# Attention scores from two products over 128 rows instead of three, with queries and keys rearranged for it, in a cross-attention and mixture-of-experts kernel

## The reference, cut to what matters

```python
q, k, v = split(concat([layernorm(x), ctx]) @ W_qkv)      # q from x, k and v from ctx
dots    = einsum('bhqd,bhkd->bhqk', q, k) * 64 ** -0.5    # the scores, summed over d = 64
x       = x + softmax(dots) @ v @ W_out + b_out
x       = x + moe(layernorm(x))                           # 16 experts, the two best for each token
```

## Time and profile before

| | us |
|---|---|
| median of 3 runs | 596.6 (596.18 to 596.95) |
| the profiled execution | 594.73 |
| its span, first to last instruction | 592.9 |
| from the first scores of pair 3 (110.15) to those of pair 14 (393.26): eleven pairs | 283.11, so 25.74 a pair |
| mean granted clock of TensorE over the span | 0.969 of 2.4 GHz |

### The profile page before, as it was taken

The page is one execution under the profiler, slowest core; times in us unless marked ns, Lnnn a source line. Parts: engine busy times, 40 slices in busy tenths (PEclk is TensorE's granted clock), DMA queues, the critical chain, the costliest instruction groups (busy, mean ns, idle before and its releaser), DMA issues.

```text
span 592.9 us, 20076 instructions
## 1 busy us (share of the span) xinstructions
PE 521.4 (88%) x6712; PEld 445.6 (75%) x6712; DVE 521.9 (88%) x1496; ACT 481.5 (81%) x1364; POOL 464.1 (78%) x567
## 2 busy tenths in 40 slices
PE   2898999999999999999999999999866878999800
PEld 0577889898999998989898999998755656666600
DVE  5879999999999999999999999999998869877616
ACT  0897999999999999999999999999966565766600
POOL 8995766788898988989898898988884577777730
PEclk9998999999999999999999999999999898999965
DMA  9793165229306384930762393075503232333139
GB/s 272 203 319 69 14 196 194 46 51 331 91 11 180 86 264 135 325 87 12 211 209 45 66 327 88 13 230 189 120 20 83 68 90 82 105 91 96 48 128 315
DMA packets 69703, 81.64 MB, mean 138 GB/s; under 512 B 8116, under 2 KB 47564, under 8 KB 69604
## 3 DMA queue, kind: packets, MB, share of 16 engines
q1 hardware_dynamic: 56244, 67.60, 39.3%
q0 software_dynamic: 4352, 8.47, 4.3%
q10 hardware_dynamic: 9008, 4.30, 2.7%
HBM read 18.82 MB, written 46.31 MB: 110 GB/s over the span
## 4 chain that ended last, share of the span: by engine, by line
PE 71%; DVE 12%; ACT 6%; issue 5%; DMA 3%; ACTq 2%; POOL 0%; POOLq 0%; SPq 0%; DVEq 0%
PE bank L1385 17%; PE bank L1384 17%; PE bank L1386 16%; PE bank L1502 8%; PE bank L1550 5%; PE bank L1591 3%; DMA ctx_sb<-results 2%; ACTq L511 1%; ACT probs L612 1%; PE bank L1640 1%; DVE pT L1251 1%; PE bank L1624 1%; PE bank L1394 1%; PE bank L1529 1%; DVE qmax L1230 1%
## 5 line engine op out<-in xcount | busy, mean ns | idle before, releaser
L612 ACT ACTIVATE probs<-bank,nbias 128x128 f32<-128x128 f32 x512 | 146.0, 368 | 4.2
L1251 DVE TENSOR_TENSOR pT<-bank,pT 128x512 f16<-128x512 f32 x128 | 87.4, 683 | 9.1 <-ACT pT L631 6.6
L928 POOL DMA_INDIRECT results<-z,stage x72 | 71.2, 989 | 21.8 <-issue 13.4
L1230 DVE TENSOR_REDUCE qmax<-bank 128x4 f32<-128x512 f32 x128 | 87.0, 679 | 0.6 <-PE bank L1386 0.6
L1384 PE MATMUL bank<-keys,q_pad 128*128 128x128 f16 x480 | 86.6, 219 | 0.0
L1386 PE MATMUL bank<-keys,q_pad 128*128 128x128 f16 x480 | 86.6, 219 | 0.0
L1385 PE MATMUL bank<-keys,q_pad 128*128 128x128 f16 x480 | 86.6, 219 | 0.0
L814 POOL DMA_INDIRECT places<-payload,slots x64 | 65.8, 1029 | 22.5 <-issue 9.3
L1502 PE MATMUL bank<-ident,probs 128*128 128x128 f32 x512 | 78.3, 275 | 4.5 <-DVE pT L1251 3.9
L631 ACT ACTIVATE pT<-bank 128x512 f16<-128x512 f32 x128 | 78.1, 610 | 4.9 <-PE bank L1502 4.8
L1384 PE MATMUL bank<-xT,w_qkv 128*128 128x256 f16 x256 | 69.9, 273 | 1.1 <-DVE xT L974 0.8
(11 more groups left out here) (266 smaller groups left out, 1958.1 us busy)
## 6 DMA issues: line engine op xcount, KB each, us to landing
places<-z SPq DMA_DIRECT2D x8, 4160.0 KB, 14.9
q_pad<-q_nat SPq DMA_DIRECT2D x120, 128.0 KB, 2.4
stage<-places SPq DMA_DIRECT2D x64, 65.0 KB, 1.8
ctx_sb<-results SPq DMA_DIRECT2D x14, 256.0 KB, 4.7
ctx_sb<-in_ctx_dram ACTq DMA_DIRECT2D x4, 512.0 KB, 10.5
stage<-in_L_ffn_Wgu_dram SPq DMA_DIRECT2D x1, 2048.0 KB, 9.5
out_dram<-x_sb ACTq DMA_DIRECT2D x7, 256.0 KB, 5.8
stage<-in_L_xattn_W_qkv_dram SPq DMA_DIRECT2D x3, 512.0 KB, 6.3
```

The costliest lines, as they stand in the source:

```text
L612: last = nc.scalar.activation(probs[:, b, k, :], score_bank[b][:, k * P:(k + 1) * P], ACT.Exp, bias=nbias[:, b, k:k + 1], scale=exp_scale)
L928: nc.gpsimd.indirect_dma_start(out=results, out_offset=bass.IndirectOffsetOnAxis(ap=to, axis=0), in_=z[:, (q - 5) % NZ, t, :], in_offset=None,
L1230: nc.vector.tensor_reduce(qmax[:, r % 2, :], score_bank[r % 2][:, :].rearrange("p (h k) -> p h k", h=4), AX.X, ALU.max).then_inc(s["qmax_o ...
L1251: nc.vector.tensor_tensor(pT[:, r % 2, LO, :], pt_bank[:, :], pT[:, r % 2, HI, :], ALU.subtract).then_inc(s["pt_lo"], 1)
```

## The change

For pairs 1 to 15 the scores of a head become two products, both over 128 rows. `q_both` holds the high half of a head's queries in its own 64 rows and the low half in the 64 rows of the other head. `k_twice` holds the high half of the keys in both sets of rows, and `k_low` the low half of the keys in the head's own rows, with zeros in the others. So q_both x k_twice gives high x high and low x high, and q_both x k_low gives high x low.

```diff
--- before.py
+++ after.py
@@ -136,9 +136,11 @@
-        q_nat = sb("q_nat", [P, 2, 4, 2, 2, 256], F16)
-        q_pad = sb("q_pad", [P, 2, 2, 8, 256], F16)
-        keys = sb("keys", [P, 2, 2, 8, 256], F16)
+        q_nat = sb("q_nat", [P, 4, 2, 2, 256], F16)
+        q_both = sb("q_both", [P, 2, 8, 256], F16)
+        k_twice = sb("k_twice", [P, 2, 8, 256], F16)
+        k_low = sb("k_low", [P, 2, 8, 256], F16)
+        keys = sb("keys", [P, 2, 8, 256], F16)
...
-        DIRECT = (1, 4, 6)
+        DIRECT = (1, 4, 7)
         VIA = [t for t in range(8) if t not in DIRECT]
...
+        def first_item(t, half):
+
+            return (k_twice if t % 4 >= 2 else q_both)[:, half, blocks_of(t), :]
+
+        def qk_item(t, half):
+
+            if t % 4 < 2:
+                return q_nat[:, blocks_of(t).start // 2, half, :, :]
+            return keys[:, half, blocks_of(t), :]
...
+                def ready(t, low):
+
+                    if t in DIRECT:
+                        sp.wait_ge(s["act_split" if low else "act_high"], direct_before(q, t) + 1)
+                    else:
+                        sp.wait_ge(s["qk_split" if low else "qk_high"], copied_before(q, t) + 1)
...
+                halves_of = [tuple(slice(64 * k, 64 * k + 64) for k in (odd, 1 - odd)) for odd in range(2)]
                 for t in (4 * g, 4 * g + 1):
-                    if t in DIRECT:
-                        sp.wait_ge(s["act_split"], direct_before(q, t) + 1)
-                    else:
-                        sp.wait_ge(s["qk_split"], copied_before(q, t) + 1)
-                    blk = 4 * g + 2 * (t % 2)
-                    for odd in range(2):
-                        rows = slice(64 * odd, 64 * odd + 64)
-                        sp.dma_start(q_pad[rows, :, odd, blk:blk + 2, :],
-                                     q_nat[rows, q % 2, blk // 2, :, :, :]).then_inc(q_moved[g], 16)
+                    ready(t, True)
+                for odd, (own, other) in enumerate(halves_of):
+                    move(q_both, (own, own), q_nat, HI)
+                    move(q_both, (own, other), q_nat, LO)
+                for t in (4 * g + 2, 4 * g + 3):
+                    ready(t, False)
+                for odd, (own, other) in enumerate(halves_of):
+                    move(k_twice, (own, own), keys, HI)
+                    move(k_twice, (own, other), keys, HI)
+                for t in (4 * g + 2, 4 * g + 3):
+                    ready(t, True)
+                for odd, (own, other) in enumerate(halves_of):
+                    move(k_low, (own, own), keys, LO)
...
-                    wait(act, "score_mm", q * 8 - 8)
-                    if t in (1, 4) and q > 2:
-                        act.wait_ge(q_moved[t // 4], 64 * (q - 2))
+                    if t in (1, 4) and q > 1:
+                        act.wait_ge(q_moved[t // 4], 160 * (q - 1))
...
-            nc.gpsimd.memset(q_pad[64:128, :, 0], 0.0).then_inc(s["pad_zero"], 1)
+            nc.gpsimd.memset(k_low[64:128, 0], 0.0).then_inc(s["pad_zero"], 1)
...
-            nc.gpsimd.memset(q_pad[0:64, :, 1], 0.0).then_inc(s["pad_zero"], 1)
+            nc.gpsimd.memset(k_low[0:64, 1], 0.0).then_inc(s["pad_zero"], 1)
...
-                if t == 0:
-                    wait(pool, "score_mm", q * 8 - 8)
-                if t in (0, 5) and q > 2:
-                    pool.wait_ge(q_moved[t // 4], 64 * (q - 2))
+                if t in (0, 5) and q > 1:
+                    pool.wait_ge(q_moved[t // 4], 160 * (q - 1))
...
+                    to = score_bank[r % 2][:, k * P:(k + 1) * P]
                     if p == 0:
-
-                        a = [q_nat[rows, par, blk // 2, h, k % 2, tok] for h in range(2)]
-                        b = [keys[rows, par, h, blk, tok] for h in range(2)]
+                        a = [q_both[rows, h, blk, tok] for h in range(2)]
+                        b = [k_twice[rows, h, blk, tok] for h in range(2)]
+                        last = three(to, a[HI], a[LO], b[HI], b[LO])
                     else:
-                        a = [q_pad[:, h, odd, blk, tok] for h in range(2)]
-                        b = [keys[:, par, h, blk, tok] for h in range(2)]
-                    last = three(score_bank[r % 2][:, k * P:(k + 1) * P], a[HI], a[LO], b[HI], b[LO])
+                        nc.tensor.matmul(to, q_both[:, odd, blk, tok], k_twice[:, odd, blk, tok], start=True, stop=False)
+                        last = nc.tensor.matmul(to, q_both[:, odd, blk, tok], k_low[:, odd, blk, tok], start=False, stop=True)
                 last.then_inc(s["score_mm"], 1)
...
-                            pe.wait_ge(q_moved[r // 2], 64 * p)
+                            pe.wait_ge(q_moved[r // 2], 160 * p)
```

More of the change, by code:

```diff
@@ L252, in direct_before, with blocks_of @@
             return (q - 1) * len(DIRECT) + sum(k < t for k in DIRECT)
[L254 to L259, removed]
+        def blocks_of(t):
+            blk = 4 * (t // 4) + 2 * (t % 2)
+            return slice(blk, blk + 2)
+        def first_item(t, half):
[4 more added lines that the diff above has]
+            return keys[:, half, blocks_of(t), :]
         def by_two(m):
@@ L418, in move_q, with move @@
                 sp.wait_ge(s["score_mm"], q * 8 - 2 + 2 * g)
-                for t in (4 * g, 4 * g + 1):
-                    if t in DIRECT:
-                        sp.wait_ge(s["act_split"], direct_before(q, t) + 1)
-                    else:
-                        sp.wait_ge(s["qk_split"], copied_before(q, t) + 1)
-                    blk = 4 * g + 2 * (t % 2)
-                    for odd in range(2):
-                        rows = slice(64 * odd, 64 * odd + 64)
-                        sp.dma_start(q_pad[rows, :, odd, blk:blk + 2, :],
-                                     q_nat[rows, q % 2, blk // 2, :, :, :]).then_inc(q_moved[g], 16)
+                def ready(t, low):
[3 more added lines that the diff above has]
+                        sp.wait_ge(s["qk_split" if low else "qk_high"], copied_before(q, t) + 1)
+                def move(to, rows, source, half):
+                    some, k = ((2 * g, 2) if source is q_nat else (4 * g, 4))
+                    from_rows = source[rows[0], some:some + k, half] if source is q_nat else source[rows[0], half, some:some + k]
+                    to_rows = to[rows[1], odd, 4 * g:4 * g + 4, :]
+                    if source is q_nat:
+                        to_rows = to_rows.rearrange("p (b i) n -> p b i n", b=2)
+                    sp.dma_start(to_rows, from_rows).then_inc(q_moved[g], 16)
+                halves_of = [tuple(slice(64 * k, 64 * k + 64) for k in (odd, 1 - odd)) for odd in range(2)]
+                for t in (4 * g, 4 * g + 1):
+                    ready(t, True)
[11 more added lines that the diff above has]
+                    move(k_low, (own, own), keys, LO)
             sp.wait_ge(s["blank_ok"], 2)
@@ L768, in split_qk @@
                 wait(pool, "qk_copied", k + 1)
-                if t == 0:
-                    wait(pool, "score_mm", q * 8 - 8)
-                if t in (0, 5) and q > 2:
-                    pool.wait_ge(q_moved[t // 4], 64 * (q - 2))
-                nc.gpsimd.tensor_tensor(qk_item(par, t, HI), each, zeros[:, :].rearrange("p (i n) -> p i n", i=2),
+                if t in (0, 5) and q > 1:
+                    pool.wait_ge(q_moved[t // 4], 160 * (q - 1))
+                nc.gpsimd.tensor_tensor(qk_item(t, HI), each, zeros[:, :].rearrange("p (i n) -> p i n", i=2),
                                         ALU.add).then_inc(s["qk_high"], 1)
                 wait(pool, "qk_high", k + 1)
-                nc.gpsimd.tensor_tensor(qk_item(par, t, LO), each, qk_item(par, t, HI), ALU.subtract).then_inc(s["qk_split"], 1)
+                nc.gpsimd.tensor_tensor(qk_item(t, LO), each, qk_item(t, HI), ALU.subtract).then_inc(s["qk_split"], 1)
             inverse_root("stat_agg", 4, mv, var_eps, rstd, "rstd_ok", 2)
@@ L1048, in first_low @@
                 dve.wait_ge(s["first_high"], t + 1)
[L1049 to L1050 removed]
+                nc.vector.tensor_tensor(first_item(t, LO), first_bank[t % 4][:, :].rearrange("p (i n) -> p i n", i=2),
+                                        first_item(t, HI), ALU.subtract).then_inc(s["first_split"], 1)
             dve.wait_ge(s["wgT_mm"], 1)
```

10 lines of the change are left out of this document (4 added, 6 removed).

## The result

The changed kernel takes 608.94 us in the median of 6 runs (607.97 to 610.93), the kernel before 596.78 us on the same chip (596.18 to 597.53): a ratio of 1.021, with a 95% interval of 1.020 to 1.023. It is slower by 12.2 us, where I had forecast 3.7 us. The sign was right, and the size lies outside my range (592 to 605).

A forecast was written before the change was run, and what follows sets the result against it. PE was taken to set the pace before, and a loop from POOL through ACT to POOL after. Terms +4.1 - 1.8 + 0.8 + 0.6 = +3.7 us on 596.6 gave 600.3 us; range for 8 in 10: 592 to 605.

The forecast's parts named there:

- The loop from POOL through ACT to POOL: Pairs 3 to 13: a ring of POOL and ACT work, 26.11 us a pair against 25.74, giving +4.1 us.
- POOL from the split of item 0 to that of item 5, 294.70 to 309.73, without a wait for another engine: 15.03: The loop's last and longest term: POOL's work from item 0 to item 5, taken to stay at 15.03 us.
- No faster PE shortens it: Claim on the 26.11 us loop: it does not pass through the scores, so PE's saving of 1.79 us a pair cannot shorten it.
- hidden, at nothing: Ten moves per group: issued every 0.64 us, landing 2.4 us after issue, 1.3 us spare at step 0, so costing nothing.
- a sign of being wrong that I had named: Stated beforehand as showing the forecast wrong: PE's longest wait ending with a DMA in step 0 or 2.
- I take half: -1.8: Pairs 1 and 2: the loop is slack, PE's gain is 3.6 us at most, and half was counted, -1.8 us.
- pair 14, +0.8: Pair 14: shift comes 1.9 us later, an earlier copy of item 5 and a lighter POOL give some back, +0.8 us.
- ahead of pair 1, +0.6: Pair 0: nothing is removed, and its last moves, now ten, may come late for pair 1, +0.6 us.
- My sentence that PE's waits should not lower it: PE's clock: claimed to stay up despite waits, since from 430 to 460 PE is busy 19.98 of 30 us at 1.00.
- the forecast's own range: The range of the main case alone: 597.5 to 603.5 us, for a loop of 25.95 to 26.4 us a pair.
- the gain gets through: Rival: the loop is shorter than 25.74 us, DVE bounds next, -8.7 and -1.8 us, 586 us; chance 0.17.
- The moves come late: Rival: moves queue behind a clearing and PE stalls at step 0 in up to seven pairs, +7 us, 607; chance 0.10.

The follow-up runs named there:

- e1_items: The kernel before with one number changed, so that POOL splits item 6 ahead of root and shift and item 7 is split directly: 645.24 against 630.97 us, ratio 1.023.
- e7_before_between: The kernel before with items 1, 4 and 7 direct and root and shift between the halves of item 6's split: 629.2 against 627.47 us, ratio 1.003.
- f1_two_products: The kernel before with the product of the queries' low halves by the keys' high halves left out from pair 1 on: 592.71 against 596.18 us, ratio 0.993.
- f4_product_again: The kernel of f3_queries_two_buffers with the first score product issued twice from pair 1 on: 601.53 against 596.18 us, ratio 1.008.
- f3_queries_two_buffers: The changed kernel with root and shift between the halves of item 6's split and q_both double-buffered by pair: 594.09 against 596.18 us, ratio 0.995.

## Why the prediction was right in kind and wrong in size

**Right: that PE's gain doesn't come through, and why.** The loop from POOL through ACT to POOL is there, and the run with the item order alone (e1_items) and the one that puts `y` back in it (e7_before_between) show it by themselves. ACT starts `y` 4.94 us behind the scores of step 7 (291.52) and not 3.93 as in the earlier trace rows, one microsecond later, as worked out. The terms of that half hold to 0.13 us.

**Wrong, the step that failed: "POOL from the split of item 0 to that of item 5, 294.70 to 309.73, without a wait for another engine: 15.03", and with it "No faster PE shortens it".** I took a stretch that had no wait while the other part of the pair was shorter, and assumed that it would keep none. It measures 15.57, with 0.56 of waiting for ACT's copy of item 5. Before, POOL ran that stretch as its own bottleneck. Afterwards the late `y` delays the exponentials of step 7, these delay PE's scores of step 1 (298.67), the transposes behind them wait 0.68 us for DVE's `pT`, and in steps 3 to 5 PE waits for DVE some tenths more. So its step 5 comes 13.06 us behind step 1, with eight products a step, where it was 12.64 with twelve; then follow item 5's projection and ACT's copy of it, for which POOL waits. The loop has a branch through PE and DVE that my sum left out. PE's own work is a small part of it: with `y` late a pair takes 26.39 us with eight products and the moves relieved, and 26.62 with twelve and the old moves. The loop term was +0.37 us a pair (26.11), where 26.39 was measured with the moves relieved and 26.49 in the changed kernel: 0.65 from this loop and about 0.1 from the moves, +8.3 and not +4.1 in pairs 3 to 13.

**Wrong: the moves "hidden, at nothing".** I took an issue at 0.64 us, a group at 5.76 from first to last issue; groups take 5.8 to 7.5. I found 1.3 us to spare at step 0 and, at step 2, 0.4 us with PE dense or about 2 more "with PE's waits". Those 2 us were the late `y`'s. With `y` back, the moves took over at 26.36 us a pair. In the changed kernel PE's waits for them are few (3.4 us in all at L1502), but the longest that it has in pairs 1 to 14 is one of them, 1.49 us at step 2 of pair 2, and that was a sign of being wrong that I had named. In five of the eleven pairs 3 to 13 the scores of step 0 or step 2 start 0.25 us after the last landing. My sentence that they cost nothing was nearly true in these pairs, and only in the shadow of the other loop. Nor are the pairs alike, as I had said: they take 25.1 to 27.3 us, and 25.0 to 27.1 with the moves relieved. Why is open.

**Wrong: pairs 1 and 2, "I take half: -1.8".** It is +1.7. The saving gives 0.3 us there (52.01 us with two products and nothing else, against 52.34), as DVE is busy for 50.95 of it; and the moves cost most of the rest: 52.47 us with the first half's moves relieved and `y` still late, 1.6 less than the 54.05 as changed. The 1.49 us named above are in these pairs.

**Right: pair 14, +0.8** (measured +1.0). **Wrong: ahead of pair 1, +0.6,** and the measured -1.4 isn't the change's either. It is the clock: pair 0 takes 25.62 us in the profile of before, with a mean granted clock of 0.93 because 3.4 us of it from 51.1 on are at 1.2 GHz, and 24.06 in that of the changed kernel at 1.00; f1_two_products, without the new moves, has 24.13 at 1.00, and f4_product_again, with them, 25.64 at 0.93. At the same clock the moves cost nothing there. Unforeseen are +2.1 from the start of pair 15 to its step 7, and 2.0 us behind it. In the first the moves are as late as in other pairs, and the clock has its part: 0.94 over that stretch, with 3.4 us at 1.2 GHz from 447.7 on, against 1.00 before. My sentence that PE's waits should not lower it rested on one row; in e7_before_between, with the old products, the clock falls in that stretch too (0.87), so these profiles don't tell whether the change has to do with it. The 2.0 us don't look like the change's: that part is 149.99 us in the kernel before and 151.85 in f1_two_products, 151.94 in the changed kernel, 152.3 in f4_product_again. Why the one profile of before is the shortest is open.

**The range.** The lower end of the forecast's own range doesn't follow from its loop: 25.95 us a pair gives 11 x 0.21 - 0.4 = +1.9, so 598.5 and not 597.5. It changes nothing here.

**The rivals.** That the gain gets through (586) was excluded from the start: even alone it is worth 3.5 us. I had put its bound at DVE, which was the right place, but 8.7 us lower than today was far too much: no kernel here had DVE busy for more than 98% of these pairs. "The moves come late" came closest in its number (607), but by another mechanism: not behind a clearing, but by SP's own issue time, and with `y`'s loop beside it. Which of the two now holds the pairs of f3_queries_two_buffers at 25.58 us, DVE and ACT (98% and 96% busy) or the loops between them, no run separates.

## What to carry to other kernels

Before pricing a saving on the busiest engine, look at the next one: with PE at 99.8%, DVE at 97% and ACT at 97% of a stretch, a saving of 7% on PE was worth 0.7%, and leaving the work out in the old kernel is the run that shows it at once. When a loop is summed from a trace, a stretch without waits is a lower bound, not a length; ask which engines its inputs come from, and what delays them once the loop is longer. When an added piece of work makes a loop longer, look which loop it was: here two of them pass through PE. And mend suspected causes together as well as singly: two loops of 26.4 us each look innocent when only the other is removed.

## What the runs showed of the hardware

PE products of 128 columns follow each other at 0.056 us when their rows are the same, 64 or 128; where a product over 64 rows follows one over 128 or the reverse, the start comes at 0.15 to 0.16 us. A step with eight products and eight such changes cost 1.27 us, more than twelve products of one kind (0.67). What the lost 0.1 us goes with is in the rows of PEld above: in a run of equal rows a load starts 0.05 us ahead of its product, behind a change of rows it starts with it. Why it isn't earlier no run here shows. The Trainium skill (TensorE: Matmul & The Clock Gate, Step-by-step: what each phase is for) says that weight loads are pulled ahead of running matmuls where their row groups don't conflict or where they go to the background weight buffer. The runs of equal rows agree with it, by the 0.05 us; it doesn't speak of a change of rows. In the table of its section Why this matters for your kernels the Trainium skill says that a single product over 32 rows takes as long as one over 128. No run here has 32 rows; with 64 the same holds within a run of equal rows (0.057 against 0.056 us).

SP's issue of a DMA is mostly 0.6 us, but four took 3.95 us in the row above. The twenty of a pair take SP 13.3 to 15.5 us in the changed kernel, a resource as real as an engine's time.
